# A three-stage decoder layer on one core: the first batch's norm, its loads and the places of the front in another order

## The reference, cut to what matters

```python
x = layernorm(x + attn(x))        # attn: x + relu(norm(x)*g+b @ K)^2 @ V, 4 heads of 64, 1024 keys
x = layernorm(x + xattn(x, ctx))  # 16 heads of 16, softmax(q k / 4 + clipped bias from frac)
x = layernorm(x + ffn(x))         # relu(x Wi + bias + top-1 LoRA) Wo
```

## Time and profile before

| what | value |
|---|---|
| median of 3 runs | 911.32 us (908.39, 911.32, 915.54) |
| the profiled execution | 915.7 us |
| its span, first to last instruction | 913.9 us |
| outside the span | 1.8 us |
| mean granted TensorE clock | 0.983 |
| busy: PE, DVE, ACT, POOL | 94%, 83%, 75%, 62% of the span |

### The profile page before, as it was taken

The page is one execution under the profiler, slowest core; times in us unless marked ns, Lnnn a source line. Parts: engine busy times, 40 slices in busy tenths (PEclk is TensorE's granted clock), DMA queues, the critical chain, the costliest instruction groups (busy, mean ns, idle before and its releaser), DMA issues.

```text
span 913.9 us, 20303 instructions
## 1 busy us (share of the span) xinstructions
PE 860.2 (94%) x7140; PEld 684.3 (75%) x7140; DVE 757.3 (83%) x2190; ACT 687.1 (75%) x1453; POOL 569.1 (62%) x748
## 2 busy tenths in 40 slices
PE   2787989999999999999999999999999999999866
PEld 1354757877888787887877787788878788788756
DVE  4868888889888888989888888988888897899842
ACT  3557888788787978878786978878797887777721
POOL 2667867766667767666676676666676766543210
PEclk9899999999999999999999999999999999999987
DMA  6223323222132222123122212213122212322100
GB/s 166 71 47 72 64 37 59 36 48 41 30 73 50 53 48 54 29 53 59 42 53 58 49 34 59 42 42 69 44 52 48 57 28 42 58 43 45 25 12 23
DMA packets 40023, 46.10 MB, mean 50 GB/s; under 512 B 10258, under 2 KB 27154, under 8 KB 39923
## 3 DMA queue, kind: packets, MB, share of 16 engines
q1 hardware_dynamic: 39922, 44.82, 24.7%
HBM read 15.42 MB, written 4.19 MB: 21 GB/s over the span
## 4 chain that ended last, share of the span: by engine, by line
PE 89%; ACT 5%; DVE 4%; issue 2%; POOL 1%; POOLq 0%; DVEq 0%; ACTq 0%
PE bank L224 21%; PE bank L268 12%; PE bank L349 12%; PE bank L411 10%; PE bank L340 6%; PE bank L256 6%; PE bank L361 6%; PE bank L257 6%; PE bank L288 2%; PE bank L418 2%; PE bank L371 2%; ACT P L562 1%; ACT R L510 1%; ACT STG L489 1%; PE bank L245 1%
## 5 line engine op out<-in xcount | busy, mean ns | idle before, releaser
L962 POOL TENSOR_TENSOR R<-R 128x512 f32<-128x512 f32 x212 | 223.2, 1053 | 90.4 <-ACT R L510 89.5
L973 POOL TENSOR_SCALAR U<-DP,alph 128x512 f32<-128x512 f32 x256 | 187.4, 732 | 124.7 <-DVE NM L773 77.1
L562 ACT ACTIVATE P<-T,NM 128x256 f32<-128x256 f32 x512 | 232.3, 509 | 3.6 <-DVE NM L773 3.6
L766 DVE SCALAR_TENSOR_TENSOR bank<-DN,alph,bank 128x512 f32<-128x512 f32 x256 | 190.9, 746 | 38.6 <-PE bank L340 36.8
L773 DVE CUSTOM_DVE_ANT_0 T<-bank,U 128x256 f32<-128x256 f32 x512 | 197.0, 422 | 9.0 <-DVE bank L766 0.2
L510 ACT ACTIVATE R<-bank 128x512 f32<-128x512 f32 x256 | 152.1, 598 | 56.8 <-PE bank L257 47.5
L489 ACT ACTIVATE STG<-bank 128x512 f32<-128x512 f32 x256 | 153.0, 598 | 51.2 <-PE bank L349 48.7
L349 PE MATMUL bank<-ident,P 128*128 128x128 f32 x1024 | 155.8, 275 | 4.3 <-ACT STG L489 3.8
L349 PEld LDWEIGHTS bank<-ident,P 128*128 128x128 f32 x1024 | 118.5, 140 | 23.4 <-ACT P L562 8.3
L268 PE MATMUL bank<-R,VS 128*32 128x512 f32 x1024 | 126.9, 614 | 3.3 <-DVE R L722 3.3
L256 PE MATMUL bank<-SK,KH 128*128 128x512 f32 x256 | 113.6, 444 | 6.9 <-DVE SK L716 5.7
(11 more groups left out here) (165 smaller groups left out, 1851.6 us busy)
## 6 DMA issues: line engine op xcount, KB each, us to landing
QS<-QK SPq DMA_DIRECT2D x384, 64.0 KB, 2.3
XG<-in_x SPq DMA_DIRECT2D x16, 256.0 KB, 2.7
CT<-in_ctxT SPq DMA_DIRECT2D x16, 256.0 KB, 2.9
out<-XO SPq DMA_DIRECT2D x16, 256.0 KB, 2.5
FK<-in_frac SPq DMA_DIRECT2D x16, 128.0 KB, 3.1
STG<-in_wiT SPq DMA_DIRECT2D x2, 512.0 KB, 4.2
STG<-in_woT SPq DMA_DIRECT2D x2, 512.0 KB, 4.3
STG<-in_kT SPq DMA_DIRECT2D x2, 256.0 KB, 4.2
```

The lines of the kernel that those rows point to most:

```text
L562: eng.activation(P[n % NP][:, cs], T[n % NT][:, cs], ACT.Exp, bias=NM[:, n % 8, q:q + 1], scale=-1.0).then_inc(s_ex, 1)
L766: eng.scalar_tensor_tensor(out=L[:, :], in0=dn[:, :], scalar=alph[:, 16 + h:17 + h], in1=L[:, :], op0=ALU.mult, op1=ALU.add).then_inc(s_t1, 1)
L962: eng.tensor_tensor(r[:, :], r[:, :], r[:, :], ALU.mult).then_inc(s_sqp, 1)
L973: eng.tensor_scalar(U[n % NU][:, :], dp[:, :], alph[:, h:h + 1], 0.0, ALU.mult, ALU.add).then_inc(s_u, 1)
```

## The change

No tile, size or count of instructions changes, and no `first`, `step` or `late`. What changes:

- SyncE issues the loads of `ln_g` and `ln_b` ahead of the two loads of the keys.
- On VectorE the keys' low half KL was the first instruction; it now stands behind the first batch's stats, centring and gain.
- `skh(0)` and `skl(0)` stand ahead of the halves of the v and k weights on both engines.
- GpSimd's first memset of QS[0] now waits for `s_x0`, the centring of batch 0.
- bqk and alph are scaled right behind Wk's low half instead of behind `centred(1)`; the q scaling moves from before square(0,0) to behind square(0,2), Wq's and Wo's high half from before relu(0,0) and behind relu(0,2) to behind relu(0,3).
- `bias_o` moves from behind scores(0,4) to behind scores(0,9), and boB on VectorE from behind square(0,5) to behind square(0,7) and `stats` of batch 1.
- On ScalarE Wp0's and Wp1's high halves move from behind relu(0,10) to behind relu(0,13) and relu(0,15); lb and wb move from behind relu(1,4) and relu(1,5) to behind relu(1,1) and relu(1,2); `ch(0)` goes ahead of relu(1,4), and `x1(0)` from behind relu(1,6) to behind relu(1,5).
- On VectorE Wp1's low half and Wi0's move ahead of square(1,0), `cl(0)` ahead of square(1,6). On TensorE scores(1,8) goes ahead of kp(0), scores(1,9) ahead of qp(0), scores(1,13) ahead of vp(0).
- SyncE loads frac and ctx of batch 0 ahead of lb and wb instead of behind them; the LB row copies go later. GpSimd's memsets of QS[1] go earlier, `plus(X1b)` of batch 0 later, and a handful of first-batch steps of the later stages (ov, x2, rsqrt c and d, centred d) shift by a step or some.

```diff
@@ scalar
-                for b, _ in due(g, -1223, early=-61, late=1):
+                for b, _ in due(g, -1223, early=-59, late=1):
                     skh(b)
...
-                if g == -2410:
+                if g == -1269:
                     weight("v", W["v"][0][:, :, :], view(512, 1, 128, 2))
-                if g == -1352:
+                if g == -1231:
                     weight("k", W["k"][0][:, :, :], view(512, 2, 128, 2))
-                if g == -1175:
+                if g == -1089:
                     act.wait_ge(s_wqs, 1)
                     weight("q", W["q"][0][:, :, :], view(512, 0, 128, 2))
...
-                if g == -714:
+                if g == -722:
                     weight("p0", WP[0][:, 0:4, :], view(1024, 1, 128, 4))
-                if g == -730:
+                if g == -625:
                     weight("p1", WP[0][:, 4:8, :], view(1024, 2, 128, 4))
...
-                for b, u in due(g, -1139, 16, 36, early=28, late=3):
+                for b, u in due(g, -1139, 16, 36, early=-80, late=3):
                     relu(b, u)
@@ vector
-            weight("kT", KL[:, :], stage(1024, 0), KH[:, :])
             for g in GRID:
...
-                if g == -2045:
+                if g == -2448:
                     dve.wait_ge(d_x[0], 16)
                     stats("a", 0, XG[0])
-                for b, _ in due(g, -1432, early=-205, late=70):
+                for b, _ in due(g, -1432, early=-275, late=70):
                     dve.wait_ge(s_xnT, b)
                     centred("a", b, XN, XG[b % 2], s_x0)
-                if g == -1537:
+                if g == -1665:
                     first_gain()
+                if g == -1571:
+                    weight("kT", KL[:, :], stage(1024, 0), KH[:, :])
...
-                for b, _ in due(g, -1226, early=-117, late=13):
+                for b, _ in due(g, -1226, early=-260, late=13):
                     skl(b)
...
-                if g == -759:
+                if g == -1314:
                     dve.wait_ge(d_small, 160)
...
-                if g == -932:
+                if g == -855:
                     dve.wait_ge(s_bvo, 1)
@@ gpsimd
-                if g == -1710:
+                if g == -1998:
+                    pool.wait_ge(s_x0, 2)
                     eng.memset(f(QS[0][:, 0, :, :]), 0.0).then_inc(s_qz, 1)
@@ sync
             load_x(0)
+            spread(gB[:, :], a["ln_g"], d_ln)
+            spread(bB[:, :], a["ln_b"], d_ln)
             eng.dma_start(stage(1024, 0)[0:64, :], a["kT"]).then_inc(d_w["kT"], 16)
             eng.dma_start(stage(1024, 0)[64:128, :], a["kT"]).then_inc(d_w["kT"], 16)
-            spread(gB[:, :], a["ln_g"], d_ln)
-            spread(bB[:, :], a["ln_b"], d_ln)
             eng.dma_start(VS[:, :, :], a["v"].rearrange("(c p) d -> p c d", p=128)).then_inc(d_v, 16)
```

More of the change, by code:

```diff
@@ L438, in _ @@
             for g in GRID:
-                for b, _ in due(g, 810, early=-5, late=-16):
+                for b, _ in due(g, 810, early=-11, late=-16):
                     ovT(b, 0)
-                for b, u in due(g, -5, 16, 39, early=4, late=6):
+                for b, u in due(g, -5, 16, 39, early=5, late=6):
                     logits(16 * b + u)
@@ L648, in _ @@
                     act.wait_ge(s_lbz, 1)
                     weight("lb", LB[0:96, :], stage(1024, 2)[0:96, :])
-                if g == -291:
+                if g == -419:
                     weight("wb", IH[0:1, 0:2, :], view(1024, 2, 1, 2))
-                for b, _ in due(g, -307, early=-42, late=-49):
+                for b, _ in due(g, -307, early=-60, late=-49):
                     ch(b)
-                for b, _ in due(g, -247, early=7, late=23):
+                for b, _ in due(g, -247, early=19, late=23):
@@ L662, in _ @@
                     vv(b)
-                for b, _ in due(g, 1099, early=-24, late=242):
+                for b, _ in due(g, 1099, late=242):
                     act.wait_ge(s_fi, 4 * b)
                     high("x2T", b, X2H, s_x2T, s_x2h)
-                for b, _ in due(g, 1207, early=-10, late=354):
+                for b, _ in due(g, 1207, early=-12, late=354):
                     gs(b)
-                for b, _ in due(g, 1275, early=-15, late=663):
+                for b, _ in due(g, 1275, early=4, late=663):
@@ L841, in y3 @@
                 stats("d", b, X2b)
-            weight("kT", KL[:, :], stage(1024, 0), KH[:, :])
             for g in GRID:
-                for b, _ in due(g, 8, early=3, late=-32):
+                for b, _ in due(g, 8, early=-6, late=-32):
                     differences(b)
-                for b, _ in due(g, 955, early=-10, late=32):
+                for b, _ in due(g, 955, early=-22, late=32):
                     y2(b)
@@ L915, in _ @@
                     cl(b)
-                for b, _ in due(g, -260, early=16, late=18):
+                for b, _ in due(g, -260, early=23, late=18):
                     low("x1T", b, X1L, X1H, s_x1h, s_x1l)
-                for b, _ in due(g, -224, early=-2, late=14):
+                for b, _ in due(g, -224, early=5, late=14):
                     projected("kp", b, 2, 2, s_kh, s_kl)
-                for b, _ in due(g, -160, early=-58, late=-22):
+                for b, _ in due(g, -160, early=-41, late=-22):
@@ L921, in _ @@
                     projected("qp", b, 1, 0, s_qh, s_ql)
-                for b, _ in due(g, 1106, early=9, late=-4):
+                for b, _ in due(g, 1106, early=-9, late=-4):
                     low("x2T", b, X2L, X2H, s_x2h, s_x2l)
-                for b, _ in due(g, 1212, early=34, late=37):
+                for b, _ in due(g, 1212, early=21, late=37):
                     gating(b)
-                for b, _ in due(g, 1275, early=-28, late=787):
+                for b, _ in due(g, 1275, early=-35, late=787):
@@ L927, in _ @@
                     ull(b)
-                for b, u in due(g, -1135, 16, 38, early=-3, late=9):
+                for b, u in due(g, -1135, 16, 38, early=-14, late=9):
                     if on_dve(b, u):
@@ L981, in _ @@
             for g in GRID:
-                for b, u in due(g, -17, 16, 40, early=9, late=-8):
+                for b, u in due(g, -17, 16, 40, early=-5, late=-8):
                     positive(16 * b + u)
-                for b, _ in due(g, -343, early=6, late=14):
+                for b, _ in due(g, -343, early=-48, late=14):
                     rsqrt("b", b)
@@ L1020, in _ @@
                     plus(X1b[b % 2], X1, boB, s_x1b)
-                for b, _ in due(g, 1383, early=123, late=634):
+                for b, _ in due(g, 1383, early=-17, late=634):
                     pool.wait_ge(s_x2, 2 * b + 2)
@@ L1025, in _ @@
                     plus(X2b, X2, woB, s_x2b)
-                for b, u in due(g, -1113, 16, 39, early=16, late=4):
+                for b, u in due(g, -1113, 16, 39, early=-18, late=4):
                     if not on_dve(b, u):
@@ L1140, in _ @@
                                   f(IL[0:1, 0:2, :])).then_inc(d_lb, 16)
-                for b, u in due(g, 82, 4, 125, early=-23, late=-107):
+                for b, u in due(g, 82, 4, 125, early=-117, late=-107):
                     restack(4 * b + u)
@@ L1144, in _ @@
                     load_f(b)
[L1145 removed]
+                if g == -1733:
                     load_x(1)
@@ L1150, in _ @@
                     load_c(b)
-                for b, _ in due(g, 2379, early=424, late=754):
+                for b, _ in due(g, 2379, early=277, late=754):
                     sp.wait_ge(s_xo, 2 * b + 2)
```

155 lines of the change are left out of this document (77 added, 78 removed).

## The result

The changed kernel takes 908.28 us (median of 20 runs, 904.75 to 911.48), the kernel before 911.67 us beside it (20 runs, 907.78 to 915.85). The ratio is 0.9956, with a 95% interval of 0.9939 to 0.9974: faster by 3.4 us in the medians and by 4.0 in the ratio, which is under half a per cent. The forecast was 904.7, 6.6 less than before. The direction was right and the time lies inside the range; the gain was a little over half of the forecast one.

What follows compares the result with a forecast made beforehand. TensorE was taken to bound the steady part, leaving 34.7 us of idle time in the front. The restack's gain, 63.84 - 7.2 + 0.6 = 57.2, gave 6.6 us: 911.3 - 6.6 = 904.7, range 899 to 910.

Steps and rivals of the forecast that it cites:

- The walk: Front, from x's landing to the first restack: step-by-step start times, with the restack forecast at 57.2 against 63.84.
- the prediction's first paragraph: Whole kernel: no step depends on absolute time, so whatever the front gains, the end comes that much earlier.
- Centring at 0.8: VectorE, batch 0: with the memset waiting, two centring instructions take 0.8 us instead of 2.2.
- The keys' price of 3.0: Start loads: putting the spreads ahead of the keys lands the keys 3.0 us later, at 9.3 instead of 6.28.
- The wait for fT: VectorE before av(0,0): scaling bqk and alph waits for fT until 16.3, costing about 1 us of the 5.3.
- lb and wb at 0.6: ScalarE, ahead of relu(1,2) and relu(1,3): they delay av(1,0) by up to 2 us, all but 0.6 hidden.
- Scores inside the projections: TensorE before the restack: scores(1,8) and (1,9) cost 0.2 to 0.5 us more before q.
- The port rule: VectorE and GpSimd's shared ports: a write-only memset blocks a tensor_scalar, but is free beside the gain and KL.
- Rival 1: The saving grows: av(0,3) fast (1.7) and no collision at norm b's factor (1.9); 10.2 us, 901.1; chance 0.20.
- Rival 2: Front: VectorE's squares meet GpSimd's more often, clock low for av(0,0) and (0,1); gain 2.5 us, 908.8; chance 0.18.
- Rival 3: Start's gain swallowed: the logits wait for something unmoved, such as loads; time stays at 911; chance 0.07.
- Rival 4: boB late behind square(0,7) delays p0's and p1's loads and skh(1); front loses about 2 us, 913; chance 0.05.

Runs made afterwards that it cites:

- the two profiles of after: The changed kernel profiled twice, unedited the second time: spans 903.0 and 904.0 us; timed 908.28, then 908.18 us.
- the repeated profile of before: The kernel before, unedited, profiled and timed anew against its own twin: span 907.7 us, timed 909.75 us, ratio 0.9976.
- the run with the memset free: The changed kernel with GpSimd's first memset of QS[0] no longer waiting for the centring: 909.37 us, one execution.
- keys-first run: The changed kernel with the keys' two loads again ahead of the spreads of ln_g and ln_b: 911.93 us, one execution.
- the added matmuls: Unread matmuls in TensorE's idle gaps: changed kernel 902.0 us, changed kernel with four places mended 899.86, kernel before 904.24.

## Why the prediction was half right

**The walk was right.** Predicted and found, in the two profiles of after: scores(0,0) at 13.2, found 13.37 and 13.49; av(0,0) at 20.1, 19.61 and 19.89; av(0,1) at 24.1, 24.44 and 24.72; av(0,2) at 29.3, 29.17 and 30.34; scores(1,0) at 36.4, 36.02 and 37.19; the restack at 57.2, 56.47 and 57.70. That the front's shift goes to the end held like for like: 4.4 at the restack, 4.6 at the 14th load, 4.7 at the end. It does not hold for any two executions, as the prediction's first paragraph has it: between the first two profiles the shift is 7.4 at the restack, 8.1 at the 14th load and 10.9 at the end, because the 42.4 or 44.0 us between two loads of x and the tail of 202.3 or 205 us differ from one execution of the same kernel to the next.

**The step that failed** is the sentence ahead of the sum: "All sums are made on the profiled execution ..., which is 4.4 above the median shown; I carry the gain over to the median." The profiled execution was long because of its own clock: of the 3.0 us at the restack 1.6 are av(0,2) itself (3.48 against 1.92) and 0.4 av(0,3) (3.64 against 3.26), while 0.2 were there at scores(0,0) already. The times after were forecast as absolute starts and subtracted from that execution's starts, so its 3.0 us of bad luck at the restack were counted as gain. With the repeated profile as the base the same walk gives 60.86 - 57.2 = 3.7, so 907.6; measured were 908.3. What the sum had wrong is its size: 6.6, where profiles and timed runs of one clock show 3.4 to 4.7. The three run times shown (908.39, 911.32, 915.54) carried the warning: the profiled 915.7 matched the longest, and av(0,2) of 3.48 beside two av of 1.92 was a row to ask of, not to take as given. In the terms of the sum: the 7.2 us at scores(1,0) should have been 5.4 (41.81 - 36.4), and the way from there to the restack is 1.2 shorter in the repeated profile of before (19.05 against 20.21), so that the sum becomes 5.4 - 0.6 - 1.2, about 3.7.

**Terms, by steps.** Centring at 0.8: 0.73 found. The keys' price of 3.0: 3.2. The wait for fT: mis-sized, and its reason fell. I let fT be issued at 13.39 as before; it is issued at 12.22 (12.00 to 12.31 in the nine profiles with the spreads ahead, 12.73 to 13.43 in the five with the keys ahead). The wait was 0.59, and 0.28 in the repeated profile, not about 1, and in the first one in part given back by alph's scaling (1.07 beside GpSimd's square, alone 0.23). lb and wb at 0.6: about the right net size (1.3 lost, 0.9 given back) by luck, since the mechanism was wrong. Scores inside the projections: 0.4, right.

**The port rule.** The gain beside the memset took 0.69 after and 0.69 where no memset ran beside it (the run with the memset free, at 8.20), while the two centring instructions beside memsets took 2.21. That is what the Trainium skill ("SBUF — State Buffer", Who interferes with whom) states: a GpSimd memset, which only writes, can block VectorE's tensor_scalar, but not an instruction with two SBUF inputs.

**The rivals.** Rival 1 (the saving grows) did not come by itself: av(0,3) stayed slow and norm b's factor grew to 3.04 instead of shrinking. But its condition was the right one: with the gap before scores(1,0) filled the clock stays, av(0,3) is fast, and with the other gaps filled too 6 us come. Rival 2 (the packed front collides, 908.8) came nearest to the time, but mostly by luck: its low clock for av(0,0) and (0,1), 3.1 of its 4.1 us, did not happen. Its collisions did: the two profiles of the changed kernel differ by 1.2 us at av(0,2), where VectorE's centring of batch 1 takes 2.35 against 1.46 and the two squares behind it 2.37 against 1.28 beside GpSimd's work, and norm b's factor cost 1.3. Rival 3 (swallowed by unmoved loads) fell: the shift is there at the restack, and the keys-first run hands its 2.1 us through. Rival 4 (boB late) fell: boB ran at 25.27, before it had run at 25.71, and no step to av(0,0) was later.

**Still open.** Why one execution of the same program keeps the clock at 30 to 40 us and the next does not; which of its slow places make up the group of before's runs at 914 and more; and the 0.8 us between av(0,2) and av(0,3) that the changed kernel needs more than before (7.57 against 6.77), with another 0.8 from there to av(1,0) (8.57 against 7.80), which no single run isolates.

## What to carry to other kernels

Before a forecast subtracts starts from a profile, set that execution's time against the run times: if it stands with the longest, find the rows that are long only by a low clock and take them out of the base, or profile once more. In a front bound by chains, look at the av or matmul rows behind each of TensorE's gaps: where they show the lower clock, filling the gap with work that nothing reads gave more here, in the medians (6.2 and 7.2 us), than all the moves of the change. An experiment of one execution is read step by step, with the clock beside each stretch, and not at its end: with the keys first the end was 7.1 us later for 2.1 us of the chain. Load first what the longest chain needs first, even at the price of delaying a bigger load by 3 us (2.1 us here).

## What the hardware showed that was not expected

- One program, one core, the same instructions: run times in groups 3 to 6 us apart. Three things were read from the profiles: whether av(0,2) ran in 1.92 or 3.48 us; whether the second and third later load of x stand 42.4 or 44.0 us apart (granted clock of 105 to 125 us 1.00 in before again, but 0.83 in the second half of it in the first profile of before); and a tail of about 202.3 or about 205 us, with a granted clock from 850 us on of 0.94 with the short one (after, both repeats, the memset free) and 0.87 to 0.89 with the long one (the seven other profiles without added matmuls). With the added matmuls the tail was 201.2 in all three kernels, at 0.95 to 0.97.
- More work, less time: the added matmuls bring 6.2 us in the changed kernel and 7.2 in the one before (911.45, measured beside it, to 904.24), and spreads shrink to 3.4, 1.4 and 0.8 us, each of six runs.
- Two GpSimd instructions on 128x1 numbers took 1.40 to 3.04 us beside VectorE's instructions with two SBUF inputs, against 0.50 in the next batch, and a chain waited for them. At up to 2.5 us it is dearer than the centring beside the memsets (2.22 against 0.73).
- The order of the first DMA issues changes when later ones are issued: with the spreads ahead of the keys SyncE reached fT at 12.00 to 12.31 us, with the keys ahead at 12.73 to 13.43, though the same transfers stood before it.
